# Row scales computed ahead of the clips and with one division, in an arccos-attention and expert-mixing kernel

## The chip, the cores and the metric

One core of a Trainium2 chip runs the whole program. The metric is the device time of one execution in microseconds (us). The kernel before was timed three times: 5250.75, 5248.96 and 5244.81, median 5248.96. One more execution was profiled: it took 5246.95, and the profile's span, in which all times below are counted, is 5245.3.

## What is computed

```python
cos = einsum('bhsd,bhtd->bhst', l2norm(q), l2norm(k))       # B=2, 16 heads of 16, S=2048
g_dist = arccos(clip(cos, -1 + 1e-7, 1 - 1e-7))
attn_score = (1 + g_dist) ** -3.2
n_r = attn_score.sum(-1); n_c = attn_score.sum(-2)
k_tilde = attn_score / n_r[..., :, None] / n_c[..., None, :]
probs = k_tilde / maximum(k_tilde.sum(-1, keepdims=True), 1e-12)
x = x + (probs @ v) @ w_out.T + b_out                       # attention, on layernorm(x)
# then, on layernorm(x) = u: softmax over 16 experts, the top two kept as gates g
x = x + u + sum_e g_e (u @ Wr_e.T + br_e) + shared experts
```

The kernel does not build `probs`. With the scores A (keys on the partitions), it sums over the keys, for every query, three things: the values over n_c (`raw`, 16 rows), 1/n_c (row HD, called `den`) and 1 (row HD + 1, called `nrow`, which is n_r). A query's output is then `raw` times a scale

s = (1/n_r) / max(den * (1/n_r), 1e-12).

This number, one for each head and query, is what the change is about. Multiplied by n_r above and below it is s = 1 / max(den, 1e-12 * n_r).

## The kernel before, in words

**The stages.** A first stage normalizes the rows and makes q, k and v. The second holds the attention of 32 heads (16 of each batch). The last stage does the output projection and the experts of the second batch. The second and last are separate blocks of code, each engine having its own instruction stream, with semaphores between them.

**The second stage** works through 64 tiles n = 4k + m, two for each head; period k has the tiles m = 0 to 3, that is two heads. A tile is 8 blocks of 128 keys by 2048 queries, in one half of the buffer `X`. Each tile goes through this chain:

- TensorE makes the cosines (L821) into two banks of PSUM; VectorE's `clip` (L965) writes them, clipped, into `X`, 16 instructions for a tile;
- GpSimd's `square` (L1166) squares them in place, 8 instructions, each released by the clips of its block;
- ScalarE's `logs` (L1193, two pieces of four blocks, each released by four squares) and `halves` (L1204) follow;
- TensorE makes the cosines again, VectorE's `mult` (L979) multiplies them in, ScalarE's `angles` (L1212), then `scores` (L1220, and L1224 in two pieces);
- VectorE's `values` (L986 to L992) sums each half and scales the values; TensorE's `add` (L846) sums over the keys; after a head's second tile VectorE copies the sums out (`evac`, L1127) and SyncE's queue stores them to `head_out`.

The order is written out by hand. At tile (k, m) VectorE does `values` of that tile, `mult` of the next, `evac` where m is odd, and `clip` of the tile after the next. ScalarE does `scores` of that tile, then `logs`, `halves` and `angles` of the next.

**Work beside the second half of the heads.** From period SIDE = 8 on, the first batch's 16 heads are complete, and each period also takes 256 rows of it through projection and experts. VectorE's part at m = 0 is `side_residual`: L1018 multiplies `side_raw` with `side_scale` (both in SBUF, in the room of the used-up `V`), TensorE projects (L875, L877), L1020 adds the residual from PSUM, L1024 and L1027 take mean and variance. ScalarE waits for L1027 at m = 1, ahead of its `logs`, to take the inverse deviation (L1231, L1233).

In periods 9 to 15 `side_residual` stands ahead of the clips. In period 8 it stands at the end of tile (8, 0), behind the clips, because its scales must first be made, once for all 16 heads:

- SyncE's queue waits for the heads' sums, loads `side_den` and `side_nrow` (L738), and waits for the scales;
- VectorE's `side_scales` makes them (L1008 to L1012, 64 partitions by 512), each step waiting for the one before (`link`);
- SyncE's queue stores them to `row_scale` (L741), waits for the store, starts three loads of expert weights (L713), then `side_rows`: two loads of raw sums (L723), two of scales spread over the rows (L725) and one of rows of x (L728); behind these it loads the stacks for the next head (L225, L230).

**The last stage** begins with the same for the second batch: the sums are loaded (L1359), then raw sums (L1364) and x (L1373); VectorE makes the scales (L1535 to L1539, 128 partitions by 256); the queue stores them (L1380), waits, loads them spread out (L1369); VectorE multiplies (L1547) and TensorE begins (L1420). From there to the end TensorE works through 16 row tiles.

Of the kernel before, what the change touches and what calls it, by code (L numbers as in the profile page):

```python
# [5 lines left out]
def pre_ln_arccos_attention_moe_kernel(nc, x, w_qkv, b_qkv, w_out, b_out, centroids, expert_biases,  # L6
# [8 lines left out]
    ALU = mybir.AluOpType  # L15
# [22 lines left out]
    TINY = 1e-12  # L38
# [15 lines left out]
    with ctx:  # L54
# [6 lines left out]
        def sem(name):  # L61
            return ctx.enter_context(nc.semaphore(name))
# [524 lines left out]
        side_den, side_nrow, side_scl = (room[0:4 * H, i * 512:(i + 1) * 512] for i in range(3))  # L587
# [26 lines left out]
        def halves(m):  # L614

            return [(c, h) for c in range(*CHUNKS.get(m, (0, 0))) for h in range(2)]
# [7 lines left out]
        side_scl_ok = sem("side_scl_ok")  # L624
# [67 lines left out]
        def has(k, m):  # L692

            return not (isinstance(k, int) and 4 * k + m >= NB)

        def starts(k, m):

            return isinstance(k, int) and k == SIDE and m == 0

        def ends(k, m):  # L700

            return isinstance(k, int) and 4 * k + m == NB - 1

        with nc.Block() as block:
# [252 lines left out]
            def _(dve):  # L957
# [10 lines left out]
                def mult(k, m, i):  # L968

                    n = 4 * k + m  # L970
                    first = mults(n, i) - PER
                    for piece, (a, b) in enumerate(HALF_PIECES):
                        if i == a:

                            dve.wait_ge(half_ok, n * len(HALF_PIECES) + piece + 1)
                    for j in range(PER):
                        dve.wait_ge(cos_ps, first + j + 1)
                        part = X[:, m % 2, i, j * CW:(j + 1) * CW]
                        nc.vector.tensor_tensor(part, ps_cos[j % 2], part, ALU.mult).then_inc(cos_ok, 1)  # L979
# [14 lines left out]
                                                "p o t d -> p (o t) d"),  # L994
                                            vp[:, a:b, HD:HD + 1].broadcast_to([P, b - a, HD]), ALU.mult).then_inc(vp_ok, 1)

                SCALE_STEPS, PAIR_STEPS = 4, 24
                steps = [0]

                def link(ins):  # L1000
                    steps[0] = steps[0] + 1
                    ins.then_inc(side_step, 1)
                    dve.wait_ge(side_step, steps[0])

                def side_scales():

                    dve.wait_ge(side_sums, 32)
                    link(nc.vector.reciprocal(side_nrow, side_nrow))  # L1008
                    link(nc.vector.tensor_tensor(side_den, side_den, side_nrow, ALU.mult))
                    link(nc.vector.tensor_scalar_max(side_den, side_den, TINY))  # L1010
                    link(nc.vector.reciprocal(side_den, side_den))
                    nc.vector.tensor_tensor(side_scl, side_den, side_nrow, ALU.mult).then_inc(side_scl_ok, 1)  # L1012

                def side_residual(k):

                    t2 = k - SIDE
                    dve.wait_ge(side_in, (t2 + 1) * 80)
                    nc.vector.tensor_tensor(side_raw, side_raw, side_scale, ALU.mult).then_inc(side_attn, 1)  # L1018
                    dve.wait_ge(side_y, t2 + 1)
                    link(nc.vector.tensor_tensor(rows2[:, :, :], ps_misc.rearrange("p (a d) -> p a d", a=2),  # L1020
                                                 rows2[:, :, :], ALU.add))
                    for h in range(2):
                        steps[0] = steps[0] + 1
                        nc.vector.bn_stats(s_stat[:, h, :], rows2[:, h, :]).then_inc(side_step, 1)  # L1024
                    hold(dve, side_step, steps[0])
                    for h in range(2):
                        nc.vector.bn_aggr(s_mean[:, h, :], s_stat[:, h, :]).then_inc(side_var, 1)  # L1027

                def side_normal(k):

                    t2 = k - SIDE

                    dve.wait_ge(side_inv, t2 + 1)
                    link(nc.vector.tensor_tensor(s_tmp, s_inv, s_inv, ALU.mult))
                    link(nc.vector.scalar_tensor_tensor(s_tmp, s_mean[:, :, 1], LN_EPS, s_tmp, ALU.add, ALU.mult))
                    link(nc.vector.tensor_scalar(s_tmp, s_tmp, -0.5, 1.5, ALU.mult, ALU.add))
                    link(nc.vector.tensor_tensor(s_inv, s_inv, s_tmp, ALU.mult))
                    for h in range(2):
                        nc.vector.tensor_scalar(side_u[:, h, :], rows2[:, h, :], s_mean[:, h, 0:1],
                                                s_inv[:, h:h + 1], ALU.subtract, ALU.mult).then_inc(side_u_ok, 1)  # L1040

                    dve.wait_ge(side_u_ok, (t2 + 1) * 2)
                    link(nc.vector.tensor_tensor(rows2[:, :, :], rows2[:, :, :], side_u, ALU.add))
                    dve.wait_ge(side_u_ps, t2 + 1)
                    nc.vector.tensor_copy(u2_t[:, :, :, :], ps_misc.rearrange("p (h c n) -> p h c n", h=2, c=KC)
                                          ).then_inc(side_ut, 1)
                    dve.wait_ge(side_l_ps, t2 + 1)
                    logits = ps_misc[:, 0:2 * NR].rearrange("p (h e) -> p h e", h=2)
                    link(nc.vector.reduce_max(s_top, logits, AX.X))
                    nc.vector.tensor_tensor(s_exp, logits, spread(s_top), ALU.subtract).then_inc(side_l_ok, 1)  # L1050
# [41 lines left out]
                def side_work(k, m):  # L1092
                    if m == 0:
                        side_residual(k)
                    if m == 1:
                        side_normal(k)
                    if m == 2:
                        side_choose(k)
# [12 lines left out]
                def emit(k, m, beside):  # L1111
                    todo = halves(m) if beside == "tail" else []
                    if ends(k, m):
                        for c, h in todo:
                            side_gather(k, c, h)
                        todo = []
                    for piece in range(len(EXP_PIECES)):
                        values(k, m, piece)
                    if has(k, m + 1):
                        for i in range(BT):  # L1120
                            mult(k, m + 1, i)
                    if m % 2 == 1:
                        head = 2 * k + m // 2
                        dve.wait_ge(sum_ps, (head + 1) * KT)

                        wait(dve, head_stored, head * 16)
                        nc.vector.tensor_copy(evac[:, :], ps_sum).then_inc(sum_ok, 1)  # L1127
                    if beside == "tail" and not starts(k, m):
                        if m == 0:
                            steps[0] = SCALE_STEPS + (k - SIDE) * PAIR_STEPS  # L1130
                        side_work(k, m)
                    for i in range(BT):
                        if has(k, m + 2):
                            clip(k, m + 2, i)
                        for c, h in todo[i:i + 1]:
                            side_gather(k, c, h)
                    for c, h in todo[BT:]:
                        side_gather(k, c, h)
                    if beside == "weights":
                        weights(k, m)  # L1140
                    if starts(k, m):
                        side_scales()
                        assert steps[0] == SCALE_STEPS
                        side_work(k, m)
                    if beside == "tail" and m == 3 and isinstance(k, int) and k == SIDE:
                        assert steps[0] == SCALE_STEPS + PAIR_STEPS
# [129 lines left out]
        den = carve([256])  # L1276
        nrow = carve([256])
        scl = carve([256])
# [37 lines left out]
        scale_ok = sem("scale_ok")  # L1316
# [31 lines left out]
        with nc.Block() as block:  # L1348
# [176 lines left out]
            def _(dve):  # L1525
                count = [0]

                def link(ins):
                    count[0] = count[0] + 1
                    ins.then_inc(chain3, 1)  # L1530
                    dve.wait_ge(chain3, count[0])


                dve.wait_ge(t_sums, 64)
                link(nc.vector.reciprocal(nrow, nrow))  # L1535
                link(nc.vector.tensor_tensor(den, den, nrow, ALU.mult))
                link(nc.vector.tensor_scalar_max(den, den, TINY))
                link(nc.vector.reciprocal(den, den))  # L1538
                nc.vector.tensor_tensor(scl, den, nrow, ALU.mult).then_inc(scale_ok, 1)  # L1539

                def scaled(k, j):

# [145 lines left out]
```

## Time and profile before

| what | value |
|---|---|
| timed, median of 3 | 5248.96 us (5244.81 to 5250.75) |
| the profiled execution | 5246.95 us; its span 5245.3 us |
| ScalarE (ACT) busy | 4835.3 us, 92% |
| VectorE (DVE) busy | 4118.7 us, 79% |
| TensorE (PE) busy | 3091.7 us, 59% |
| GpSimd (POOL) busy | 1817.5 us, 35% |
| DMA, mean | 24 GB/s |

Shares over the whole span mix stages with different limits. For a change at two places what counts is which engine was late there, and who waited for it; that is in the timelines and the waits. In a timeline a row is a run of like instructions on one engine; the brackets give the idle time ahead of it and what ended that.

### The profile page before, as it was taken

Reading aid. Unit: us, or ns where it says so; the run is one execution under the profiler, and the core shown is the slowest. Engines: PE = TensorE matmul, PEld = TensorE weight load, DVE = VectorE, ACT = ScalarE, POOL = GpSimd, SP = SyncE. Lnnn points to the kernel's source line nnn. Section 1 sums busy time; section 2 is a strip of 40 time slices with the busy share of each in tenths; the row PEclk is TensorE's granted clock in tenths of the full one; section 3 lists DMA queues with packets and bytes.
Section 4 is the critical chain, followed back from the end, with each engine's and each line's share of the span. In section 5 each row is a group of like instructions: output and inputs, shape, how many; then the busy total and the mean of one; then the engine's idle time right before and its main releaser. Section 6 shows DMA issues by size and latency. Waiting matters only on the chain. (4 is left out here: it accounts for less than half of the span.)

```text
span 5245.3 us, 37144 instructions
## 1 busy us (share of the span) xinstructions
PE 3091.7 (59%) x10544; PEld 797.6 (15%) x10678; DVE 4118.7 (79%) x3989; ACT 4835.3 (92%) x1266; POOL 1817.5 (35%) x548
## 2 busy tenths in 40 slices
PE   8644456545554554555446565655666555665699
PEld 4200001001010000000011111111111111111244
DVE  7777777777877777787778888887888888887566
ACT  5899999999999999999989999999999999999421
POOL 0324443334433344433433444334433343334000
PEclk9867766666667666766667778686867878687799
DMA  2200000000000000000000101010100101010200
GB/s 89 65 10 12 18 18 18 11 13 18 18 18 14 10 10 10 10 9 3 12 29 26 34 26 36 14 40 10 48 14 26 34 26 36 14 40 2 84 32 13
DMA packets 71845, 128.16 MB, mean 24 GB/s; under 512 B 9654, under 2 KB 46937, under 8 KB 71706
## 3 DMA queue, kind: packets, MB, share of 16 engines
q1 hardware_dynamic: 70554, 122.50, 7.4%
q0 software_dynamic: 1152, 4.19, 0.3%
q14 instruction: 100, 0.82, 0.1%
q8 instruction: 39, 0.64, 0.1%
HBM read 96.77 MB, written 29.88 MB: 24 GB/s over the span
## 5 line engine op out<-in xcount | busy, mean ns | idle before, releaser
L1166 POOL TENSOR_TENSOR X<-X 128x2048 f32<-128x2048 f32 x504 | 1798.2, 3602 | 2824.3 <-DVE X L965 2824.3
L821 PE MATMUL psum<-stacks 128*128 128x512 bf16 x3962 | 1620.4, 500 | 847.4 <-DVE X L979 451.7
L979 DVE TENSOR_TENSOR X<-psum,X 128x1024 f32<-128x1024 f32 x1024 | 1190.1, 1218 | 421.0 <-ACT X L1204 385.2
L846 PE MATMUL psum<-X,vp 128*32 128x512 f32 x4096 | 720.0, 868 | 1159.0 <-DVE vp L992 1159.0
L986 DVE TENSOR_REDUCE ncol<-X 128x4 f32<-128x8192 f32 x128 | 1111.5, 8683 | 365.9 <-ACT X L1224 364.8
L965 DVE TENSOR_SCALAR X<-psum 128x1024 f32<-128x1024 f32 x1024 | 1192.0, 1218 | 30.5 <-DVE rows L1086 24.7
L1212 ACT ACTIVATE X<-X 128x4096 f32<-128x4096 f32 (+1 forms) x192 | 898.0, 4740 | 21.4 <-DVE X L979 21.4
L1204 ACT ACTIVATE X<-X 128x4096 f32<-128x4096 f32 x256 | 904.8, 3605 | 0.7
L1224 ACT ACTIVATE X<-X 128x8192 f32<-128x8192 f32 x128 | 892.8, 7022 | 2.0
L1220 ACT ACTIVATE X<-X,consts 128x16384 f32<-128x16384 f32 x64 | 892.9, 13951 | 0.8
L1193 ACT ACTIVATE X<-X,consts 128x8192 f32<-128x8192 f32 x126 | 889.7, 7109 | 0.0
L821 PEld LDWEIGHTS psum<-stacks 128*128 128x128 bf16 x4096 | 254.8, 103 | 2254.1 <-DVE X L979 1201.6
L846 PEld LDWEIGHTS psum<-X,vp 128*32 128x32 f32 x4096 | 162.3, 151 | 1691.9 <-DVE vp L992 862.4
L861 PE MATMUL psum<-V,u_t 128*128 128x512 f32 (+1 forms) x576 | 265.6, 591 | 4.4 <-DVE rows L1086 4.4
L1455 PE MATMUL psum<-X 128*128 128x512 f32 (+1 forms) x576 | 244.8, 575 | 0.0
L1622 DVE SCALAR_TENSOR_TENSOR X<-psum,X 128x256 f32<-128x256 f32 x240 | 104.5, 479 | 72.1 <-PE psum L1455 67.1
L1086 DVE SCALAR_TENSOR_TENSOR rows<-psum,gate,rows 128x256 f32<-128x256 f32 x256 | 123.0, 480 | 21.2 <-PE psum L861 16.7
L861 PEld LDWEIGHTS psum<-V,u_t 128*128 128x128 f32 x576 | 111.3, 196 | 101.5 <-issue 75.2
L1455 PEld LDWEIGHTS psum<-X 128*128 128x128 f32 x576 | 106.1, 190 | 111.4 <-issue 97.8
L519 PE MATMUL psum<-X 128*128 128x512 f32 (+1 forms) x256 | 101.7, 521 | 0.7 <-ACT X L320 0.7
L1508 ACT ACTIVATE X<-psum 18x128 f32<-18x128 f32 x16 | 4.3, 267 | 91.7 <-PE psum L1446 91.7
L1204 ACT ACT_TABLE_LOAD x64 | 82.1, 1283 | 1.1
(167 smaller groups left out, 1125.4 us busy)
## 6 DMA issues: line engine op xcount, KB each, us to landing
V<-expert_w SPq DMA_DIRECT2D x64, 512.0 KB, 3.6
stacks<-qk_parts SPq DMA_DIRECT2D x256, 64.0 KB
qk_parts<-X SPq DMA_DIRECT2D x96, 128.0 KB, 2.0
stacks<-qk_parts SPq DMA_DIRECT2D x64, 192.0 KB
head_out<-evac SPq DMA_DIRECT2D x32, 256.0 KB, 2.1
expert_w<-u_t SPq DMA_DIRECT2D x17, 256.0 KB, 2.6
X<-in_L_attn_x_dram POOLq DMA_DIRECT2D x8, 512.0 KB, 4.3
stacks<-qk_parts SPq DMA_DIRECT2D x32, 128.0 KB
```

The costliest lines, as they stand in the source:

```text
L821: return nc.tensor.matmul(dst, stacks[:, 1, buf, keys:keys + P], stacks[:, 0, buf, q0:q0 + n], start=True, stop=True)
L846: mm = nc.tensor.matmul(ps_sum[32 * j:32 * j + 32, :], vp[:, i, :], X[:, m % 2, i, j * 512:(j + 1) * 512], start=(m % 2 == 0 and i == 0), ...
L861: mm = nc.tensor.matmul(dst, u2_t[:, h, kc, :], w_ring[c % 3][:, kc, 0:wide], start=(kc == 0), stop=(kc == KC - 1 and wide == 2 * D))
L965: nc.vector.tensor_scalar(X[:, m % 2, i, j * CW:(j + 1) * CW], ps_cos[j % 2], -CLIP, CLIP, ALU.max, ALU.min).then_inc(cos_ok, 1)
L979: nc.vector.tensor_tensor(part, ps_cos[j % 2], part, ALU.mult).then_inc(cos_ok, 1)
L986: nc.vector.reduce_sum(ncol[:, a:b], X[:, m % 2, a:b, :], AX.X).then_inc(sums_ok, 1)
L1166: nc.gpsimd.tensor_tensor(own, own, own, ALU.mult).then_inc(square_ok, 1)
L1193: nc.scalar.activation(own, own, ACT.Ln, bias=one_c, scale=-1.0).then_inc(log_ok, 1)
L1204: nc.scalar.activation(own, own, ACT.Sigmoid, scale=-0.5).then_inc(half_ok, 1)
L1212: nc.scalar.activation(own, own, ACT.Arctan).then_inc(atan_ok, 1)
L1220: nc.scalar.activation(own, own, ACT.Ln, bias=theta_c, scale=-2.0).then_inc(log2_ok, 1)
L1224: nc.scalar.activation(own, own, ACT.Exp, scale=POWER).then_inc(score_ok, 1)
```

## The change

Two chains of five VectorE instructions (two reciprocals, two products, one maximum) become two instructions each: one that forms max(nrow * TINY, den), and a reciprocal of it. The first chain is also moved, within tile (8, 0): from behind the clips of tile (8, 2) to ahead of them. `side_residual`, which reads the scales, stays behind the clips. `SCALE_STEPS` counts the linked steps.

```diff
-                SCALE_STEPS, PAIR_STEPS = 4, 24
+                SCALE_STEPS, PAIR_STEPS = 1, 24
...
                     dve.wait_ge(side_sums, 32)
-                    link(nc.vector.reciprocal(side_nrow, side_nrow))
-                    link(nc.vector.tensor_tensor(side_den, side_den, side_nrow, ALU.mult))
-                    link(nc.vector.tensor_scalar_max(side_den, side_den, TINY))
-                    link(nc.vector.reciprocal(side_den, side_den))
-                    nc.vector.tensor_tensor(side_scl, side_den, side_nrow, ALU.mult).then_inc(side_scl_ok, 1)
+                    link(nc.vector.scalar_tensor_tensor(side_den, side_nrow, TINY, side_den, ALU.mult, ALU.max))
+                    nc.vector.reciprocal(side_scl, side_den).then_inc(side_scl_ok, 1)
...
                         side_work(k, m)
+                    if starts(k, m):
+                        side_scales()
+                        assert steps[0] == SCALE_STEPS
                     for i in range(BT):
                         if has(k, m + 2):
                             clip(k, m + 2, i)
...
                     if starts(k, m):
-                        side_scales()
-                        assert steps[0] == SCALE_STEPS
                         side_work(k, m)
...
                 dve.wait_ge(t_sums, 64)
-                link(nc.vector.reciprocal(nrow, nrow))
-                link(nc.vector.tensor_tensor(den, den, nrow, ALU.mult))
-                link(nc.vector.tensor_scalar_max(den, den, TINY))
-                link(nc.vector.reciprocal(den, den))
-                nc.vector.tensor_tensor(scl, den, nrow, ALU.mult).then_inc(scale_ok, 1)
+                link(nc.vector.scalar_tensor_tensor(den, nrow, TINY, den, ALU.mult, ALU.max))
+                nc.vector.reciprocal(scl, den).then_inc(scale_ok, 1)
```

## Rows read from the trace of the kernel before

**Rows 1.** Waits of ScalarE, whole run: us in total, times, longest us.

```profile
ACT X L1212 <- DVE X L979: 21.4, 12, 2.5
ACT small L1231 <- DVE small L1027: 20.2, 1, 20.2
```

**Rows 2.** Busy time of PE, PEld, DVE, ACT, POOL in one stretch, clock, DMA.

```profile
2694.00:4900.00 2206.00, 1330.43 (x4538) 338.28 (x4604) 1838.07 (x1667) 2181.65 (x442) 828.00 (x232) 0.77 0.09 28
```

**Rows 3.** Timeline of ScalarE, tiles (8, 1) and (8, 2): start us, us.

```profile
2659.33 13.95 ACT L1224 ACTIVATE X<-X 128x8192 f32<-128x8192 f32 x2
2693.45 0.29 ACT L1231 ACTIVATE small<-small,consts 128x2 f32<-128x2 f32 x1 [20.17 <-DVE small L1027]
...
2693.89 14.12 ACT L1193 ACTIVATE X<-X,consts 128x8192 f32<-128x8192 f32 x2
...
2724.72 14.05 ACT L1212 ACTIVATE X<-X 128x8192 f32<-128x8192 f32 x3 [1.26 <-DVE X L979]
```

**Rows 4.** Timeline of VectorE, from the clips of tile (8, 2) on.

```profile
2638.23 18.18 DVE L965 TENSOR_SCALAR X<-psum 128x1024 f32<-128x1024 f32 x16
2656.33 3.33 DVE L1008 RECIPROCAL V<-V 64x512 f32<-64x512 f32 x1
2659.70 2.89 DVE L1009 TENSOR_TENSOR V<-V 64x512 f32<-64x512 f32 x1
2662.62 3.71 DVE L1010 TENSOR_SCALAR V<-V 64x512 f32<-64x512 f32 x1
2666.36 3.35 DVE L1011 RECIPROCAL V<-V 64x512 f32<-64x512 f32 x1
2669.74 0.68 DVE L1012 TENSOR_TENSOR V<-V 64x512 f32<-64x512 f32 x1
2686.04 0.69 DVE L1018 TENSOR_TENSOR V<-V 128x512 f32<-128x512 f32 x1 [15.62 <-DMA rows<-in_L_attn_x_dram]
2691.55 0.69 DVE L1020 TENSOR_TENSOR rows<-psum,rows 128x512 f32<-128x512 f32 x1 [4.82 <-PE psum L877]
...
2693.61 8.69 DVE L986 TENSOR_REDUCE ncol<-X 128x4 f32<-128x8192 f32 x1 [0.19 <-issue]
```

**Rows 5.** Timeline of SyncE's queue around the first batch's scales.

```profile
2568.45 1.22 SPq L738 DMA_DIRECT2D V<-head_out  x2
2670.45 0.51 SPq L741 DMA_DIRECT2D row_scale<-V  x1
```

**Rows 6.** Timeline of GpSimd in the same stretch.

```profile
2640.65 29.13 POOL L1166 TENSOR_TENSOR X<-X 128x2048 f32<-128x2048 f32 x8 [43.73 <-DVE X L965]
```

**Rows 7.** All eight L1020: what ended VectorE's idle time before them, us, times.

```profile
  PE psum L877: 23.8, 8
```

**Rows 8.** L992 and L1086, all: ns min/median/max, first and last start.

```profile
L992 DVE TENSOR_TENSOR vp<-V,vp x128: 224/226/1201, 277.7 to 4920.4; 128x64 f32<-128x64 f32 x128
...
L1086 DVE SCALAR_TENSOR_TENSOR rows<-psum,gate,rows x256: 472/483/486, 2813.1 to 4899.5; 128x256 f32<-128x256 f32 x128
```

**Rows 9.** Timeline at the head of the last stage, VectorE and SyncE's queue.

```profile
4933.14 0.46 SPq L1373 DMA_DIRECT2D X<-in_L_attn_x_dram  x1
4933.55 1.75 DVE L1535 RECIPROCAL X<-X 128x256 f32<-128x256 f32 x1 [6.84 <-DMA X<-head_out]
4935.34 0.43 DVE L1536 TENSOR_TENSOR X<-X 128x256 f32<-128x256 f32 x1
4935.80 0.29 DVE L1537 TENSOR_SCALAR X<-X 128x256 f32<-128x256 f32 x1
4936.13 1.75 DVE L1538 RECIPROCAL X<-X 128x256 f32<-128x256 f32 x1
...
4938.37 1.20 SPq L1380 DMA_DIRECT2D row_scale<-X  x2
```

**Rows 10.** L1622, a multiply-add of two tensors and a scalar: ns min/median/max.

```profile
L1622 DVE SCALAR_TENSOR_TENSOR X<-psum,X x240: 473/477/486, 4962.9 to 5241.2; 128x256 f32<-128x256 f32 x120
```

**Rows 11.** Busy times by stretch at the last stage's head; DMA share, GB/s last.

```profile
4935.50:4937.00 1.50, 0.00 (x0) 0.00 (x0) 1.43 (x3) 0.00 (x0) 0.00 (x0) 0.50 0.99 302
```

## Prediction

> **What bounds the kernel now.** I read the shares first: ScalarE is busy for 92% of the span, more than any other. So I asked where ScalarE stands still inside the attention stage, with its waits [rows 1]. There are only two kinds: 21.4 us in 12 short waits for VectorE's `mult` (L979), none over 2.5, and one single wait of 20.2 us for L1027, the last step of `side_residual`. ScalarE does the rest back to back: from that wait to its last score it is busy for 2181.65 of 2206 us [rows 2]. A microsecond taken from the single wait therefore moves all that follows, as no other engine sets the pace behind it.
>
> Then the timelines of both engines. ScalarE ends the scores of tile (8, 1) at 2659.33 + 13.95 = 2673.28 and stands until 2693.45 [rows 3]. VectorE is what it waits for [rows 4]: clips until 2656.4, the five scale instructions until 2670.42, idle for 15.62 us until the last load of `side_rows` has landed, L1018 at 2686.04, 4.82 us for TensorE's projection, L1020 and the statistics until 2693.4. The reader is to see that the scales, a round trip through DRAM and the residual stand in a row on VectorE, with nothing beside them. The 1.26 us wait at L1212 [rows 3] is the same event's echo: `values` of (8, 1) began only at 2693.61 [rows 4], together with ScalarE's logs and not 7 us ahead of them.
>
> The last stage's head is a bare chain too: sums loaded, five instructions, store [rows 9], loads, with all engines waiting for it. The scale chain lasts from 4933.55 to the store's issue at 4938.37, 4.82 us.
>
> **First edit, the chain in period 8.** Removed there: two products, a maximum and a reciprocal. Left: a reciprocal of 3.35 (L1011) and the new instruction. The trace has none of that form in this shape; L1012, two tensors of the same shape in and one out, took 0.68 [rows 4], and a multiply-add of 128x256 took 0.477 beside 0.43 for a product of that shape [rows 9, 10], so 0.68 to 0.75. I take 0.70, and 4.1 us for both with the 0.04 between linked steps. The longer values of L1009 and L1010 (2.89 and 3.71) don't apply (in the last stage, where GpSimd is idle, a half as long maximum took 0.29 [rows 9]): GpSimd's squares ran then (2640.65 to 2669.8) and in the new place they don't; it had been idle for 43.73 us when the first clip released it [rows 6].
>
> **The move.** The chain now starts at 2638.2 and ends at 2642.3. Its input was requested at 2568.45 [rows 5], 70 us earlier, so the wait for the sums is free. Queued behind it on VectorE are the 16 clips; they end at 2642.3 + 18.2 = 2660.5, 4.1 us later than before. Behind the clips are TensorE's cosines and GpSimd's squares: the squares start 4.1 later and end at 2669.8 + 4.1 = 2673.9, the fourth at about 2659.3. ScalarE's first piece of logs needs the fourth at 2673.8, the second piece needs the eighth 14.12 / 2 = 7.1 us later [rows 3], at 2680.9. The margins are 14.5 and 7.0 us, so the 4.1 are covered. Uncovered, each microsecond would cost one.
>
> SyncE's queue issued the store at 2670.45, 0.03 after the scales, and VectorE could begin L1018 15.62 us after them. All of this (store, its landing, three weight loads, five loads of rows) moves with the scales: 2642.3 + 15.6 = 2657.9, 2.6 us before the clips end. The loads of stacks that stand behind in this queue come 28 us earlier too; the `mult` they wait for is over at 2638.2, so they hold nobody.
>
> So the residual starts at 2660.5. Before, it took 7.4 us with the 4.82 us wait for the projection. Over the eight periods this wait is 23.8 us [rows 7], the other seven being (23.8 - 4.8) / 7 = 2.7 each; period 8's long one came after TensorE had stood for 32 us, and now it will not have. That gives 5.3 to 7.4, so an end at 2665.8 to 2667.9. ScalarE comes at 2673.28. It does not wait: 20.17 gained. `values` of (8, 1) then starts within 2 us of its scores, whose first half is ready at 2666.3, so the 1.26 at L1212 goes as well. Sum of the middle: 21.4 us.
>
> What comes late next? L1018 now runs while the squares run. L1009, a product of two SBUF tensors like it, took 2.2 us more than L1012 there, and L992 was once 1.201 against 0.226 [rows 8]. A square takes 29.13 / 8 = 3.6 us, so the wait is 0 to 3.6. The residual's end becomes 2671.5 at worst, still 1.8 ahead of ScalarE: I cost it at nothing. The Trainium skill states in "SBUF — State Buffer", section "SBUF: two separate sides", that a VectorE instruction with two SBUF inputs and a GpSimd instruction exclude each other for a whole instruction. The trace agrees with its 2.89 against 0.68; by that rule L1018 waits and L1020, with one input in PSUM, does not.
>
> **Second edit, the last stage.** 4.82 us become 0.45 (0.43 to 0.48, [rows 9, 10]) + 0.04 + 1.75 + 0.04 = 2.3, a gain of 2.5. The queue is free, as its previous issue, the load of x, began at 4933.14 and took 0.46. But that load is then in flight: the DMA engines are 99% busy up to 4937.0 [rows 11]. The store, issued at 4935.9, meets this; before it came after it. That gives back between 0 and 1.1 us (4937.0 less 4935.9). I take 0.2, nearer to nothing since the data go only after the issue, leaving 2.3.
>
> **Sum.** 21.4 + 2.3 = 23.7 us. From the profiled execution's 5246.95 this is 5223.3; from the median it is 5225.3. I say 5224. A difference under 0.2% (10.5 us) can't be told from none here.
>
> **Rivals.**
> - *The port.* Not only L1018 but the other steps of the residual wait behind squares, up to the squares' end at about 2674.6. The residual would end near 2676.6 and the echo at L1212 would be back: 3.3 + 1.3 = 4.6 lost, 5229. For it: L1010, with one input, waited as well (3.71). Against it: the 256 multiply-adds of L1086, which have an input in PSUM and stand between the clips, never took over 0.486 [rows 8]. By the skill's rule above it would be L1018 alone, and 5224.
> - *The loads.* The store, the weights and the rows come later than 15.6 us after the scales. The queue's issues don't depend on VectorE, but the landing is bounded by nothing. There are 2.6 us before VectorE notices and 5.4 more before ScalarE does; doubled to 31 us, the residual would end near 2679 to 2681, ScalarE losing 6 to 8 and the echo 1.3: about 5232.
> - *A wait in its place.* The clips are late, and ScalarE waits for squares at 2680.9. It decides from a chain of over 11.1 us (7.0 + 4.1); at the old chain's 14.0 it costs 3 us. To use up the whole 20 us it would have to last 31. Then only the last stage's 2.3 stay: 5247, no measurable change.
> - *Slower.* The chain's wait for the sums now has 16 clips behind it, and through them GpSimd and ScalarE. If the sums landed only at 2680, 111 us after their request, the clips would end at 2702, the loads be in at 2700 and the residual end at 2708; ScalarE would begin its logs at 2708 instead of 2693.9, and with 2.3 back the time is 12 us longer, 5261. It decides from a landing at about 2668 on. Against it: these are two loads requested at 2568.45 and the queue had nothing else before 2670.
>
> **Chances.** The forecast (gain 20 to 26) 0.80; the port 0.08; the loads 0.06; a wait in its place 0.04; slower 0.02. The forecast alone spans 5221 to 5228 and, with a median of three that moves by 3 either way, 5218 to 5231. The port and part of the loads lie within 5217 to 5235, which is the range. Faster by over 0.2%: 0.93; within 0.2%: 0.05; slower: 0.02.
>
> **What the changed kernel's profile would show.** Right: no row for L1231 among ScalarE's waits; scales of two instructions, 0.7 and 3.35, right before the clips of (8, 2); L1018 right behind the clips with no idle time for a load, and longer than 0.69; the clips, squares and the logs at about 2673.8; other short L1212 waits as before, 11 of them, near 20 us in sum; the last stage's store 2.5 us after the sums. Wrong: ScalarE idle ahead of L1193 for GpSimd (clips too late), L1018 with idle time for a DMA (loads), L1020 or the statistics lengthened (port), more or longer L1212 waits later on, which would mean that TensorE or VectorE took over what ScalarE gave up.

## Result and the profile after

The changed kernel takes 5227.22 us, median of 6 (5222.35 to 5228.58); the kernel before, timed beside it, 5248.76. The ratio is 0.9958, interval 0.9947 to 0.9968: 21.5 us faster. The profiled execution's span is 5224.0, against 5245.3.

Waits of ScalarE, whole run, after. Behind the first chain the kernel's lines are 2 or 3 lower: L1210 is the old L1212, L1015 the old L1018, L1017 the old L1020, L1021 and L1024 the statistics (old L1024 and L1027):

```profile
ACT X L1210 <- DVE X L979: 19.8, 11, 3.1
```

No row for the inverse deviation is left, and there is one short wait less than in [rows 1]. ScalarE's timeline over tiles (8, 1) and (8, 2), to be set against [rows 3]:

```profile
2659.69 13.96 ACT L1222 ACTIVATE X<-X 128x8192 f32<-128x8192 f32 x2
2673.55 0.28 ACT L1229 ACTIVATE small<-small,consts 128x2 f32<-128x2 f32 x1
2673.86 0.20 ACT L1231 ACTIVATE small<-small 128x2 f32<-128x2 f32 x1
2673.97 14.12 ACT L1191 ACTIVATE X<-X,consts 128x8192 f32<-128x8192 f32 x2
...
2703.45 14.03 ACT L1210 ACTIVATE X<-X 128x8192 f32<-128x8192 f32 x3
```

No brackets: it is back to back. The angles begin at 2703.45 and not 2724.72, though this execution came to the place 0.36 us later (2659.69 against 2659.33): 21.6 us gained here. VectorE, against [rows 4] (L1008 and L1009 are now the two scale instructions):

```profile
2638.27 0.67 DVE L1008 SCALAR_TENSOR_TENSOR V<-V 64x512 f32<-64x512 f32 x1
2638.97 3.35 DVE L1009 RECIPROCAL V<-V 64x512 f32<-64x512 f32 x1
2642.24 19.26 DVE L965 TENSOR_SCALAR X<-psum 128x1024 f32<-128x1024 f32 x16
2661.42 1.56 DVE L1015 TENSOR_TENSOR V<-V 128x512 f32<-128x512 f32 x1
2667.38 0.69 DVE L1017 TENSOR_TENSOR rows<-psum,rows 128x512 f32<-128x512 f32 x1 [4.40 <-PE psum L877]
2668.11 0.75 DVE L1021 BATCH_NORM_STATS2 small<-rows 128x6 f32<-128x256 f32 x2
2669.00 0.25 DVE L1024 BATCH_NORM_AGGREGATE small<-small 128x2 f32<-128x6 f32 x2
2669.17 8.66 DVE L986 TENSOR_REDUCE ncol<-X 128x4 f32<-128x8192 f32 x1
```

The scales are two instructions ahead of the clips. L1015, the product with the scales, has no idle time ahead of it: the store and all loads went by under the clips. The residual is over at 2669.25, 4.3 us before ScalarE asks for it. GpSimd and SyncE's queue:

```profile
2644.60 28.95 POOL L1164 TENSOR_TENSOR X<-X 128x2048 f32<-128x2048 f32 x8 [46.95 <-DVE X L965]
```

```profile
2642.35 0.51 SPq L741 DMA_DIRECT2D row_scale<-V  x1
...
2648.74 0.49 SPq L728 DMA_DIRECT2D rows<-in_L_attn_x_dram  x1
```

The head of the last stage, against [rows 9]:

```profile
4911.53 0.46 SPq L1371 DMA_DIRECT2D X<-in_L_attn_x_dram  x1
4911.79 0.43 DVE L1533 SCALAR_TENSOR_TENSOR X<-X 128x256 f32<-128x256 f32 x1 [6.68 <-DMA X<-head_out]
4912.25 1.75 DVE L1534 RECIPROCAL X<-X 128x256 f32<-128x256 f32 x1
4914.03 1.19 SPq L1378 DMA_DIRECT2D row_scale<-X  x2
4917.91 1.36 SPq L1367 DMA_DIRECT2D X<-row_scale  x2
4923.38 1.43 DVE L1542 TENSOR_TENSOR X<-X 128x256 f32<-128x256 f32 x4 [9.37 <-DMA X<-row_scale]
```

The chain is 2.58 us shorter: 4911.79 to 4914.03, against 4933.55 to 4938.37. But the store is followed by the next issue only after 3.88 us. So here are the rows of before for it, which the prediction did not read:

```profile
4938.37 1.20 SPq L1380 DMA_DIRECT2D row_scale<-X  x2
4941.03 1.36 SPq L1369 DMA_DIRECT2D X<-row_scale  x2
...
4946.52 1.43 DVE L1547 TENSOR_TENSOR X<-X 128x256 f32<-128x256 f32 x4 [8.19 <-DMA X<-row_scale]
```

There it was 2.66. First scale instruction to first product (below: the head) took 12.97 us and takes 11.59, 1.4 less; and from this product to the end of the span it took 298.8 us (5245.3 - 4946.52) and takes 300.6, 1.8 more. The last stage as a whole has gained nothing. What that is, the second set of experiments asks.

### The profile page after: what moved, and what is told of

It reads as the page before. It is cut to its first block and busy times, and to the rows that moved or that the text cites. A ratio compares the mean times of both kernels' runs of the same rounds, so it can differ in the third digit from the quotient of the medians.

```text
span 5224.0 us, 37272 instructions
## 1 busy us (share of the span) xinstructions
PE 3152.8 (60%) x10678; PEld 802.5 (15%) x10678; DVE 4109.3 (79%) x3983; ACT 4835.2 (93%) x1266; POOL 1817.3 (35%) x548
## 5 line engine op out<-in xcount | busy, mean ns | idle before, releaser
L821 PE MATMUL psum<-stacks 128*128 128x512 bf16 x4096 | 1690.3, 507 | 794.0 <-DVE X L979 426.6
L846 PE MATMUL psum<-X,vp 128*32 128x512 f32 x4096 | 709.6, 856 | 1161.3 <-DVE vp L992 1161.3
L1210 ACT ACTIVATE X<-X 128x4096 f32<-128x4096 f32 (+1 forms) x192 | 898.0, 4740 | 19.8 <-DVE X L979 19.8
L846 PEld LDWEIGHTS psum<-X,vp 128*32 128x32 f32 x4096 | 160.8, 149 | 1687.3 <-DVE vp L992 866.9
L1083 DVE SCALAR_TENSOR_TENSOR rows<-psum,gate,rows 128x256 f32<-128x256 f32 x256 | 122.8, 480 | 21.6 <-PE psum L861 17.1
```

What stands on the lines that cost most here:

```text
L821: return nc.tensor.matmul(dst, stacks[:, 1, buf, keys:keys + P], stacks[:, 0, buf, q0:q0 + n], start=True, stop=True)
L846: mm = nc.tensor.matmul(ps_sum[32 * j:32 * j + 32, :], vp[:, i, :], X[:, m % 2, i, j * 512:(j + 1) * 512], start=(m % 2 == 0 and i == 0), ...
L1210: nc.scalar.activation(own, own, ACT.Arctan).then_inc(atan_ok, 1)
```

## Experiments

### Which part of the change does it

**Only period 8** (`e1_middle_only`): the changed kernel with the last stage's old chain of five.

```diff
-                link(nc.vector.scalar_tensor_tensor(den, nrow, TINY, den, ALU.mult, ALU.max))
-                nc.vector.reciprocal(scl, den).then_inc(scale_ok, 1)
+                link(nc.vector.reciprocal(nrow, nrow))
+                ...
+                nc.vector.tensor_tensor(scl, den, nrow, ALU.mult).then_inc(scale_ok, 1)
```

> The short, moved chain in period 8; the last stage's chain is the old one of five. Theory (the gain is the wait of ScalarE that went): no wait at L1229 or its like, the L1210 wait of tile (8, 2) gone too, so 21.4 us less than before, about 5227.5, as fast as the whole change within what can be measured. Rival (the last stage's 2.5 us count in full): this kernel is 2.3 to 2.5 us slower than the whole change. In the profile the last stage's scales take 4.8 us again, and the store's landing 2.7 us instead of 3.9, so the head of the last stage (first scale instruction to first product) is back at 13.0 us against 11.6.

Measured: 5228.76 us, ratio 0.9959 (0.9944 to 0.9973), the whole change's gain within what can be measured. The wait for the deviation is gone, and 11 short ones are left. From the store to the queue's next issue (below: the store) it is 2.65 us, the head 13.05.

**Only the last stage** (`e2_last_only`): the kernel before with the new chain there, the reverse edit.

> Only the last stage's chain is the new one; period 8 is as before. Theory: ScalarE waits 20.2 us at L1231 as before, the head of the last stage is 11.6 us instead of 13.0; the time is 1 to 1.5 us under before, which can't be told from nothing. Rival (the whole effect sits in the bare chain at the head of the last stage): a gain well over 10 us.

Measured: ratio 1.0 (0.999 to 1.0009), 5248.61 us. ScalarE waits 19.3 us for L1027, as before within 1 us. The head is 11.62 us, the store 4.01. From the first scale instruction to the span's end it is 311.6 us, against 311.8 before: of the 1.4 us gained in the head 0.1 to 0.2 arrive at the end.

**The short chain in the old place** (`e3_short_in_place`): the kernel before with the new chain there; here, as in the other runs, `SCALE_STEPS` follows the number of linked steps.

```diff
                 def side_scales():
                     dve.wait_ge(side_sums, 32)
-                    link(nc.vector.reciprocal(side_nrow, side_nrow))
-                    ...
-                    nc.vector.tensor_tensor(side_scl, side_den, side_nrow, ALU.mult).then_inc(side_scl_ok, 1)
+                    link(nc.vector.scalar_tensor_tensor(side_den, side_nrow, TINY, side_den, ALU.mult, ALU.max))
+                    nc.vector.reciprocal(side_scl, side_den).then_inc(side_scl_ok, 1)
```

> The two-instruction chain of period 8 in the old place, behind the clips; the last stage as before. Theory (everything there stands in a row on VectorE): the chain is 3.4 for the reciprocal plus 0.7 to 4.3 for the two-input instruction, which now meets GpSimd's squares, some 6.3 us instead of 14.1; ScalarE's wait of 20.2 falls by 7.8 to about 12.4, the idle time for the loads stays 15.6, the 1.3 us at L1212 stays; time about 5241. Rival (the shortening is what counts, the move nothing): near 5227.

Measured: 5240.82 us, ratio 0.9985 (0.9976 to 0.9995), 8 us gained. VectorE's timeline, then ScalarE's:

```profile
2638.43 18.19 DVE L965 TENSOR_SCALAR X<-psum 128x1024 f32<-128x1024 f32 x16
2656.53 2.71 DVE L1008 SCALAR_TENSOR_TENSOR V<-V 64x512 f32<-64x512 f32 x1
2659.27 3.35 DVE L1009 RECIPROCAL V<-V 64x512 f32<-64x512 f32 x1
2677.18 0.69 DVE L1015 TENSOR_TENSOR V<-V 128x512 f32<-128x512 f32 x1 [14.56 <-DMA rows<-in_L_attn_x_dram]
```

```profile
2684.23 0.29 ACT L1228 ACTIVATE small<-small,consts 128x2 f32<-128x2 f32 x1 [10.74 <-DVE small L1024]
...
2715.07 14.04 ACT L1209 ACTIVATE X<-X 128x8192 f32<-128x8192 f32 x3 [0.83 <-DVE X L979]
```

The new instruction takes 2.71 us beside the squares and 0.67 without them. The wait fell by 9.4 us, somewhat more than the 7.8 expected: the chain is 8.0 us shorter, the loads' idle time 1.1 and the wait for the projection 0.4 (4.46 against 4.82). The way through DRAM stays in the open.

**The old chain, moved** (`e4_long_moved`): the changed kernel with five instructions in the new place, the last stage as before.

> The old five-instruction chain, moved ahead of the clips; the last stage as before. Theory: with GpSimd idle the five take 3.35 + 0.68 + 0.4 to 0.7 + 3.35 + 0.68 + links = 8.7 us, so clips and squares are 4.6 us later than after the change; the squares end near 2678 and ScalarE needs the last at 2681: no wait there. The residual ends near 2673.9, when ScalarE comes at 2673.6: a wait of 0 to 2 us, and 0 to 1.3 at L1212. The move alone thus gains 18 to 21.4 us: 5228 to 5231. Rival (the shortening matters as much as the move): under 14 us gained. L1009 and L1010 take 0.68 and at most 0.7 us here, where they took 2.89 and 3.71 beside the squares.

Measured: 5230.98 us, ratio 0.9966 (0.9953 to 0.9979): some 18 us from the move alone. The interval is 11 to 25 us, so the time can't tell this from the whole change's 21.5; the rows can. VectorE, then ScalarE:

```profile
2639.09 3.33 DVE L1008 RECIPROCAL V<-V 64x512 f32<-64x512 f32 x1
2642.46 0.68 DVE L1009 TENSOR_TENSOR V<-V 64x512 f32<-64x512 f32 x1
2643.18 0.42 DVE L1010 TENSOR_SCALAR V<-V 64x512 f32<-64x512 f32 x1
...
2666.69 1.72 DVE L1018 TENSOR_TENSOR V<-V 128x512 f32<-128x512 f32 x1
...
2674.86 0.25 DVE L1027 BATCH_NORM_AGGREGATE small<-small 128x2 f32<-128x6 f32 x2
```

```profile
2675.14 0.30 ACT L1232 ACTIVATE small<-small,consts 128x2 f32<-128x2 f32 x1 [1.24 <-DVE small L1027]
...
2706.41 14.05 ACT L1213 ACTIVATE X<-X 128x8192 f32<-128x8192 f32 x3 [1.25 <-DVE X L979]
```

The same two instructions that took 2.89 and 3.71 us [rows 4] take 0.68 and 0.42 where GpSimd is idle. The residual is now 1.24 us too late, and with it the echo returns, 2.5 in all. That is what the shortening is worth once the chain is moved; in the old place it was 8.

**Three more reciprocals** (`e5_three_more`).

```diff
+                    for _ in range(3):
+                        link(nc.vector.reciprocal(side_scl, side_nrow))
                     link(nc.vector.scalar_tensor_tensor(side_den, side_nrow, TINY, side_den, ALU.mult, ALU.max))
```

> The changed kernel with three more reciprocals of the same shape (3.4 us each) ahead of its chain in period 8; their results are overwritten. It puts the clips, squares and the residual 10.1 us later. Theory (the residual is what comes late first): it ends at 2669.3 + 10.1 = 2679.4, ScalarE, there at 2673.6, waits 5.8 us for it, the L1210 wait of tile (8, 2) comes back with 1.3, and the squares, ending near 2683.7, are in time for logs that begin at 2680: 7.1 us slower than the changed kernel, 5234. Rival (the squares are what comes late first): the wait is ahead of the logs and for GpSimd, 2 to 3 us. Rival (10 us on VectorE cost 10 us): 5237, or nothing: 5227.

Measured: 5236.01 us, ratio 0.9973 (0.9963 to 0.9983). ScalarE, then GpSimd:

```profile
2679.76 0.29 ACT L1231 ACTIVATE small<-small,consts 128x2 f32<-128x2 f32 x1 [6.52 <-DVE small L1026]
2680.08 0.20 ACT L1233 ACTIVATE small<-small 128x2 f32<-128x2 f32 x1
2680.19 14.12 ACT L1193 ACTIVATE X<-X,consts 128x8192 f32<-128x8192 f32 x2
...
2711.02 14.05 ACT L1212 ACTIVATE X<-X 128x8192 f32<-128x8192 f32 x3 [1.26 <-DVE X L979]
```

```profile
2654.66 28.95 POOL L1166 TENSOR_TENSOR X<-X 128x2048 f32<-128x2048 f32 x8 [57.32 <-DVE X L965]
```

ScalarE waits for the residual and not for the squares: these end at 2683.6, the second piece of logs begins at 2687.2. 10.1 us more on VectorE cost 6.52 + 1.26 = 7.8 in these rows, and 7 in the times (14.2 us gained instead of 21.5). The margin that the move has is thus the residual's 4.3 us; 10.1 - 4.3 leaves 5.8, and the other 0.7 is the residual itself, which took 8.6 us here and 7.8 in the changed kernel.

### Where the last stage's gain goes

**The load of x behind the store** (`e6_x_behind_store`) and **behind the spread loads** (`e7_x_behind_scales`); the first is

```diff
                 load_sums(0)
-                load_x(0)
                 sp.wait_ge(scale_ok, 1)
                 for own, q in halves:
                     sp.dma_start(row_scale[H:NH, :, q].rearrange("h j s -> (h j) s"), scl[own, :]
                                  ).then_inc(scale_out, 16)
+                load_x(0)
```

> The changed kernel, with the last stage's first load of x issued behind the stores of the scales and no longer ahead of them. Theory (the store of the scales met the traffic of this load, and lost 1.2 us to it): the store's way to the next issue is 2.7 us again and not 3.9, unless x, now issued right behind it, meets the spread loads of the scales, which come next; the head of the last stage is 10.4 to 11.6 us; 0 to 1.2 us faster, 5226 to 5227. Rival (the store took longer for another reason, its own distance to the loads of raw sums): still 3.9 us.

> The same with that load issued behind the spread loads of the scales. Theory: the store takes 2.7 us again and the spread loads are undisturbed, so the first product starts 1.2 us earlier, 10.4 us after the first scale instruction; x then lands about 5.7 us behind its issue, near the moment at which the first row tile needs it, which may give up to 2 us back. 5225 to 5229. Rival (as for the other order): no shorter store.

Measured: 5228.22 us (0.9957, 0.9943 to 0.997) and 5227.58 us (the same ratio). The store takes 2.67 and 2.66 again, but the way from the spread loads' issue to the product grows from 5.47 to 7.33 and 7.40. Of the second one the rows of SyncE's queue, then of VectorE:

```profile
4916.68 1.19 SPq L1377 DMA_DIRECT2D row_scale<-X  x2
4919.34 1.36 SPq L1367 DMA_DIRECT2D X<-row_scale  x2
4920.74 0.45 SPq L1371 DMA_DIRECT2D X<-in_L_attn_x_dram  x1
```

```profile
4926.74 1.43 DVE L1542 TENSOR_TENSOR X<-X 128x256 f32<-128x256 f32 x4 [10.09 <-DMA X<-row_scale]
```

The theory on the store holds. In the five kernels with the short chain and x right ahead of the store, x being issued 2.5 us before it, the store took 3.73 to 4.35 us; in the other eight, with x 5 us ahead of it or elsewhere, 2.65 to 2.67. The hope for a better order doesn't hold: x is issued behind the spread loads here and still delays them. The heads are 12.24 and 12.31 us, longer than the changed kernel's.

**The changed kernel again** (`e8_change_again`), to compare the last three with (the run beside them, on the same chip).

> The changed kernel again, as the one to compare the next three with, on the same chip: head of the last stage (first scale instruction to first product) 11.6 us, store to next issue 3.9, TensorE's clock up some 16 us after the first product, 300.6 us from the first product to the end.

Measured: 5229.96 us, 0.9959 (0.9946 to 0.9973); head 11.48, store 3.78, first product to end 300.5.

**The load of x ahead of the last tile** (`e9_x_early`), to a view `x_first` of the same room. Only the main lines of the edit are shown.

```diff
                         for c in range(NC):
                             sp.dma_start(we_t[c], ...).then_inc(t_in, 16)
+                        sp.dma_start(x_first, x_rows[GPB * GT:(GPB + 1) * GT, :].rearrange("(j p) d -> p j d", p=P)
+                                     ).then_inc(xres_in, 16)
...
                 load_sums(0)
-                load_x(0)
```

> The changed kernel, with the last stage's first load of x issued with the expert weights before the last tile, in room that is free by then. Theory (x's traffic costs wherever it lies in this head: 1.2 us on the store, 1.9 on the spread loads): the store takes 2.7 and the spread loads at most 5.5 us, the head is 10.4 us or less. A second theory (the clock goes up about 35.5 us after the attention's last sum, whatever the head lasts): the product starts 1.2 us earlier and the clock then rises that much later after it, so half of the gain goes: 0.6 us in all, not measurable by the time. Rival to the second: the time from the first product to the end stays at 300.6.

Measured: 5228.57 us, 0.9957 (0.9943 to 0.997). The store takes 2.65, the spread loads 5.37, the head 10.26. From the product to the end it is 301.2 us, 0.6 more than in the run beside it: half of the 1.2 gained is given back. Granted clock (third number from the right) 16 to 17, and 17 to 18 us after the first product, of the run beside it and of this one:

```profile
4945.66:4946.66 1.00, 1.00 (x3) 0.32 (x2) 0.00 (x0) 0.00 (x0) 0.00 (x0) 0.69 0.00 0
4946.66:4947.66 1.00, 1.00 (x4) 0.52 (x3) 0.84 (x2) 0.00 (x0) 0.00 (x0) 1.00 0.00 0
```

```profile
4941.74:4942.74 1.00, 1.00 (x2) 0.34 (x1) 0.00 (x0) 0.00 (x0) 0.00 (x0) 0.50 0.00 0
4942.74:4943.74 1.00, 1.00 (x3) 0.36 (x2) 0.47 (x2) 0.00 (x0) 0.00 (x0) 0.59 0.00 0
```

**Three tiny instructions** (`e10_fillers`): writes to unused columns of `consts`, which gets two more for it. Removing six instructions from VectorE's program and adding three leaves it as long as in the kernels where only three were removed.

```diff
+                    for j in range(3, 6):
+                        nc.vector.memset(consts[:, j:j + 1], 0.0)
                     dve.wait_ge(side_sums, 32)
```

> The changed kernel with three tiny writes to unused constants on VectorE ahead of the scales in period 8, so that the stage's later VectorE code lies where it lies in the kernels with three instructions fewer removed. Theory (the 1.1 us that the changed kernel lost at three places in the last stage's loop come from where the code lies): the steps of 5.84 us at these places are 5.49 again, 299.5 us from first product to end. Rival (something of the scales' content or timing): 5.84 stays.

Measured: 5230.41 us, 0.9963 (0.9949 to 0.9977). The first product to the end takes 299.7 us, 0.8 less than in the run beside it: two row tiles of the loop that took 18.22 us take 17.87 (transposed rows to transposed rows, L1428), and one at the loop's turn 19.16 instead of 19.26. These two tiles took 18.22 in the five profiled kernels with VectorE's full six instructions fewer, and 17.87 to 17.91 in the eight others. So what costs here goes with how many instructions VectorE's program holds, and not with what the scales compute. That it is the place of the later code is the theory of this run; how a place could cost stays open, and so does the rest of the longer turn, 18.96 us before.

**Both** (`e11_both`): the early load of x and the three tiny instructions.

> Both of these: 1 to 2 us less than the changed kernel, 5226; at the edge of what can be told by the time, with a head of 10.4 us and loop steps of 5.49 in the profile.

Measured: 5225.8 us, ratio 0.9958 (0.9944 to 0.9971); the head is 10.29 and first product to end 300.1. Its profile gains 1.6 us over the run beside it from the first scale instruction on (310.4 against 312.0); the time can't tell that from nothing. No version beats the changed kernel by more than can be measured.

## Why the prediction was right, and where it wasn't

**The bound.** Right. ScalarE's single wait was the whole matter, and after it nothing else set the pace: `e1_middle_only` with period 8 alone has the full gain, `e2_last_only` none (the intervals reach 8 and 5 us to either side).

**The chain and its new place.** 4.1 us predicted, 4.05 measured (2638.27 to 2642.32). The clips took 19.26 us and not 18.2. TensorE had stood 4.45 us for the chain, and its granted clock was 0.59 from 2640 to 2656 (1.00 before); four of the cosines' matmuls took 2.16 us, where two took 0.60 before. With the chain behind the clips these took 18.18 and 18.19 (three kernels), with it ahead of them 18.94 to 19.27 (ten kernels). That the clock fell because TensorE stood is read from this order of events, not tested apart. That 1 us was not in the sum, and the margins took it.

**The loads** were hidden, as predicted. **The port.** L1015 took 1.56 us, 0.9 more than its 0.69 without squares, inside the 0 to 3.6; L1017 and the statistics took 0.69, 0.75 and 0.25 as before, while the squares ran on to 2673.55. So the rival in which all steps wait is refuted. Across the kernels the product with the scales took 1.55 to 1.88 us beside squares, the two-input instructions of the chain 2.71 and 2.89. A one-input one was lengthened as well: L1010 took 3.71 beside squares and 0.42 in `e4_long_moved`. The prediction counted it for the rival. The Trainium skill names in "SBUF — State Buffer", section "SBUF: two separate sides", beside two SBUF inputs, a VectorE instruction in a mode that uses both ports; that L1010 ran in such a mode no run here shows. (The rival's sum took the squares' end at 2674.6, where the prediction's own working gave 2673.9; measured was 2673.55.)

**The residual.** The wait for the projection was 4.40 us, not 2.7, inside the range but near its upper end. TensorE had stood 2.9 us and not 32, but its clock was at half (granted 0.50 from 2655 to 2665; L875's first four took 2.07 us). In the seven periods with 2.7 us the granted clock over this projection was 1.00, in period 8 before it was 0.50. So what the prediction put down to TensorE having stood goes with the level of the clock, and having stood less did not raise it in time. The residual ended at 2669.25, inside 2665.8 to 2671.5.

**The sum of the middle**: 21.4 predicted, 21.6 measured at this place. That 21.8 had also reached the last stage in this pair of profiles is in part luck: in the second execution of the changed kernel (`e8_change_again`, on another chip) it was 15.4, its short waits at L1210 being 26.9 us in sum instead of 19.8.

**A wait in its place** was placed wrongly. The prediction let it decide from a chain of 11.1 us, by the squares. In fact the residual is what comes late first: a chain of 8.6 us (`e4_long_moved`) already cost 2.5, one of 14.2 (`e5_three_more`) 7.8. The rule used, to compare each branch behind the moved work with its own deadline, was applied to the squares and to the short chain's residual, but not to the long chain's.

**The last stage** is the step that failed: "leaving 2.3". The profile has -0.5. The chain's 2.58 us are there; three things took them back. The first: the store lost 1.2 us to the load of x (predicted 0.2, at most 1.1), which `e6_x_behind_store` to `e9_x_early` show. The second, TensorE's clock, took 0.8. Its first twelve expert matmuls, before and after:

```profile
4960.24 6.04 PE L1455 MATMUL psum<-X 128*128 128x512 f32 x12
```

```profile
4937.08 6.83 PE L1453 MATMUL psum<-X 128*128 128x512 f32 x12
```

First product and clock in the two profiles: the product is 23.1 us earlier (4946.52, 4923.38), the granted clock goes from 0.50 to 1.00 21.6 us earlier (at 4961.5, a mean of 0.73 in 4961 to 4962, and at 4940.0, a mean of 0.52 in 4939 to 4940), and 21.6 is how much earlier the attention's last sums (L846) end: 4925.9 and 4904.3. In eleven of the thirteen profiles the rise kept this distance from those sums, in two (`e2_last_only`, `e6_x_behind_store`) it came 1 us later, while from the first product it was 14.6 to 17.8 us away. That is a coincidence of times; what the clock goes by was not tested. What it costs is plain: over the thirteen profiles the first row tile of the loop takes 14.13 us where the rise comes 14.6 us after the first product and 15.69 where it comes 17.8 after, 0.5 us for each microsecond, with no profile off this line by more than 0.01. The third is 1.1 us in the loop: 0.7 in the two tiles that `e10_fillers` restores, 0.4 at its turn, open. Together 1.4 - 0.8 - 1.1 = -0.5, and 21.8 - 0.5 = 21.3, the difference of the spans; the 21.8 is the distance of the first scale instructions.

**The number.** The gain was put at 23.7 us; the medians give 21.5 and the spans 21.3. In the profiles the term of the last stage was 2.8 too high and the way up to it 0.4 too low; single executions differ by more than that. The rest of the 3 us by which 5224 was low is the choice of a number below the median's own 5225.3.

## What to carry to other kernels

When one engine sets the pace, look for its single long waits and read backwards what stands in a row in front of them; work whose inputs have long been there belongs ahead of the next independent stretch, so that its way through DRAM runs under it. Then give every branch behind the moved work its own deadline, with the longest version you might put there: here the tightest was the residual, with 4.3 us. A shorter chain at a bare head is worth what the next transfer and the clock let through: here 1.4 of 2.6 us reached the first product, and 0.6 were left after the first row tile.

## What the runs showed that was not expected

- The same kernel in two profiled executions reached the last stage's first scale instruction at 4911.79 and at 4918.18. Its short waits at L1210 sum to 19.8 and 26.9 us: these waits differ by about as much as the two executions do there.
- Three tiny instructions more on VectorE, far ahead, changed two row tiles in a later loop from 18.22 to 17.87 us.
- The maximum on 64x512 (L1010) takes 0.42 us with GpSimd idle and took 3.71 beside a square of 3.6.
